# Two attention layers and two expert FFNs on one core: probabilities from block-diagonal queries, token-major experts, other load orders

## The reference

```
x = x + L0_xattn(layernorm(x), ctx, ctx)   # 32 query heads of 8 over 8 key heads; softmax(q k / sqrt(8)) v
x = x + L0_ffn(layernorm(x))               # 2 experts, 256 -> 1024 -> 256, leaky relu squared, the better expert
x = x + L1_xattn(layernorm(x), ctx)        # 16 heads of 16; q = x Wq, k and v = ctx Wkv; causal; then Wout
x = x + L1_ffn(layernorm(x))               # below
```

## Time and profile before

| | us |
|---|---|
| median of 3 runs (390.49 to 393.13) | 390.66 |
| the profiled execution | 389.83 |
| its span, first to last instruction | 387.8 |
| PE busy in it | 345.8 |
| DVE busy | 163.6 |
| ACT busy | 150.4 |
| POOL busy | 90.8 |

### The profile page before, as it was taken

The page is one execution under the profiler, slowest core; times in us unless marked ns, Lnnn a source line. Parts: engine busy times, 40 slices in busy tenths (PEclk is TensorE's granted clock), DMA queues, the critical chain, the costliest instruction groups (busy, mean ns, idle before and its releaser), DMA issues.

```text
span 387.8 us, 11733 instructions
## 1 busy us (share of the span) xinstructions
PE 345.8 (89%) x5105; PEld 282.2 (73%) x5105; DVE 163.6 (42%) x481; ACT 150.4 (39%) x349; POOL 90.8 (23%) x134
## 2 busy tenths in 40 slices
PE   2365679899998999899999999899999999996996
PEld 1234568777785887788788896788877888885784
DVE  4360473007730346088502684016364156327034
ACT  3012424332153332347142140433553666666452
POOL 6832423422342113142122430042100000200000
PEclk9999969989999999899999999999999999999899
DMA  3999000000000000000000000000000001000000
GB/s 87 288 401 365 8 1 3 3 3 2 0 3 3 3 3 2 3 3 3 0 5 3 0 1 2 5 0 2 0 2 27 3 1 32 0 0 15 14 1 29
DMA packets 7106, 12.84 MB, mean 33 GB/s; under 512 B 2576, under 2 KB 5392, under 8 KB 6288
## 3 DMA queue, kind: packets, MB, share of 16 engines
q1 hardware_dynamic: 7056, 12.10, 9.0%
HBM read 11.04 MB, written 1.05 MB: 31 GB/s over the span
## 4 chain that ended last, share of the span: by engine, by line
PE 82%; issue 6%; DVE 4%; SPq 3%; ACT 3%; POOL 1%; DMA 1%; DVEq 0%; POOLq 0%
PE Y L1243 27%; PE S L1243 27%; PE H L1243 24%; SPq L679 2%; PE S L1321 2%; DMA WKV<-in_wkv 1%; ACT PT L766 1%; PE S L1429 1%; PE S L1330 1%; POOL X L891 1%; SPq L674 1%; DVE XN L1002 0%; DVE MN L1030 0%; ACT YS L842 0%; PE S L1249 0%
## 5 line engine op out<-in xcount | busy, mean ns | idle before, releaser
L1243 PE MATMUL Y<-WP,A 128*128 128x256 f32 x256 | 64.0, 399 | 0.0
L1243 PE MATMUL H<-XT,WF 128*128 128x256 f32 x256 | 62.1, 391 | 0.0
L1243 PEld LDWEIGHTS Y<-WP,A 128*128 128x128 f32 x256 | 48.9, 199 | 8.1 <-issue 1.5
L1243 PEld LDWEIGHTS H<-XT,WF 128*128 128x128 f32 x256 | 47.9, 194 | 7.9 <-issue 1.5
L907 POOL TENSOR_TENSOR A<-R 128x512 f32<-128x512 f32 x32 | 33.2, 1040 | 61.9 <-PE Y L1243 57.5
L824 ACT ACTIVATE A<-H,B 128x256 f32<-128x256 f32 x84 | 35.6, 471 | 30.8 <-PE H L1243 30.7
L1243 PE MATMUL Y<-A,W 128*128 128x256 f32 x168 | 45.9, 383 | 0.4 <-DVE YG L1206 0.4
L1243 PE MATMUL H<-GH,W 128*128 128x256 f32 x168 | 44.6, 392 | 0.3 <-ACT GH L813 0.3
L796 ACT ACTIVATE R<-H 128x512 f32<-128x512 f32 x32 | 19.1, 598 | 47.4 <-POOL A L907 24.0
L1243 PEld LDWEIGHTS H<-GH,W 128*128 128x128 f32 x168 | 31.9, 195 | 5.7 <-issue 0.6
L1243 PEld LDWEIGHTS Y<-A,W 128*128 128x128 f32 x168 | 30.6, 192 | 6.3 <-issue 1.1
(11 more groups left out here) (171 smaller groups left out, 492.4 us busy)
## 6 DMA issues: line engine op xcount, KB each, us to landing
W<-in_w SPq DMA_DIRECT2D x2, 1344.0 KB, 9.2
WF<-in_wf SPq DMA_DIRECT2D x2, 1024.0 KB, 9.0
WP<-in_wp SPq DMA_DIRECT2D x2, 1024.0 KB, 11.1
X<-in_x SPq DMA_DIRECT2D x8, 128.0 KB, 7.5
out_dram<-X SPq DMA_DIRECT2D x8, 128.0 KB, 1.7
KR<-in_ctxT SPq DMA_DIRECT2D x4, 192.0 KB, 3.2
KR<-in_ctxT SPq DMA_DIRECT2D x8, 32.0 KB, 2.1
C<-in_ctx_in SPq DMA_DIRECT2D x1, 256.0 KB, 3.2
```

Of the source, the lines that this page charges most:

```text
L1243: return nc.tensor.matmul(o, a, b, start=start, stop=stop, skip_group_check=shared)
```

## The change

**Loads.** Rows 0 and 1 come first, then the context, rows 2 and 3 in one transfer, the keys of tiles 2 to 7, rows 4 to 7 in one transfer, and then the rest as before. The keys of tiles 0 and 1 are four transfers that ACT issues ahead of its own work.

**First attention.** After the scores POOL spreads the queries in the place of the keys (`k`, `queries0`, `Z0`), so that the second build takes 16 matmuls of 256 columns with the plain keys `KR0` as weights. The turned shifts are no longer copied by ACT: DVE multiplies them, from PSUM, with the 0/1 columns `place` into `MD0`, eight copies each of which keeps one of eight heads (`t`, `spread_shifts0`), and 8 matmuls of 512 columns with `ofbank0` add them, one for each bank, half and sequence.

**Second attention.** The same, with 4 shift and 8 score matmuls (`MD1`, `ofbank1`, `Z1`). ACT copies the keys out of PSUM, and POOL instead of DVE spreads the keys (`c`) and the queries (`k`).

**Second FFN.** The down products are token-major: `A1` stands in the array, 128 rows at a time, and the 128 columns of `W2` move, two matmuls a chunk. The gates are then a number per partition, and DVE multiplies and adds in one operation a tile. The selector matmuls, the three-part split `GS`, `YS` and `YG` are gone. The values at zero and the biases are one more product with the turned gates at the last expert (`ROWS0`), `zero_rows` makes that table with nine rows instead of eight, and a new stage `k` (`turn_sums`) turns the sum for `widen`. Constants for the selectors go, those for the new products come.

**Orders.** `COST`, `LOADED` and `URGENCY` have new numbers, so each engine's order is new. Two lines of it:

```diff
-    "ffn1": "v 38 -981 -81 -709; ln 661 727 727 220; x 460 425 492 992; i -16 -3 19 -711; r 695 118 935 143; "
+    "ffn1": "v -457 595 -279 -873; ln -550 -628 -623 -267; x 555 313 346 180; i 990 696 353 572; "
```

The core of the rest:

```diff
-            rows(0)
-            keys(0, 0, 1)
-            rows(1)
-            keys(1, 1, 2)
+            rows(0, 1)
+            rows(1, 2)
             sp.dma_start(C[:, :, :], ctx_in.rearrange("(t p) d -> p t d", p=P)).then_inc(ld_c, 16)
-            rows(2)
-            rows(3)
-            keys(2, 2, TILES)
+            rows(2, 4)
+            keys(sp, 1)
+            rows(4, 8)
             sp.dma_start(CT[:, :], ctxT).then_inc(ld_kv, 16)
...
+            keys(act, 0)
             run("act", h | {("attn0", "f"): probs0, ("attn0", "b"): values0, ("const", "e"): places0, ("attn1", "f"): probs1, ("attn1", "kv"): keys1,
...
+            def queries0(t, _):
+
+                filled(pool, "attn0", t, "h", 3)
+                read_out(pool, "attn0", t, "q", 0)
+                for c in range(DC):
+                    nc.gpsimd.tensor_tensor(Z0[:, t % 2, c, :, :], QT0[:, t % 2, c, :].unsqueeze(1).to_broadcast([P, 4, P]),
+                                            quarter0[:, :].unsqueeze(2).to_broadcast([P, 4, P]), ALU.mult).then_inc(qz_ready, 1)
...
+            def spread_shifts0(t, _):
+                b, done = filled(dve, "attn0", t, "t", 0)
+                nc.vector.tensor_tensor(MD0[:, t % 2, :, :], b[:, :].bitcast(bf16)[:, 0:P].unsqueeze(1).to_broadcast([P, 8, P]),
+                                        place[:, :].unsqueeze(2).to_broadcast([P, 8, P]), ALU.mult).then_inc(done, 1)
...
-                for j in range(8):
-                    for k in range(2):
-                        for r in range(2):
-                            i = 2 * r + k
-                            half = slice(r * S, (r + 1) * S)
-                            for bt in range(2):
-                                rows = slice(bt * S, (bt + 1) * S)
-                                mm(claims_[i][0][rows, j * S:(j + 1) * S], sel0[half, 8 * i + j, :], MT0[half, t % 2, rows],
-                                   start=(j == 0), stop=False, shared=True)
-                for j in range(8):
-                    c, r = divmod(j, 4)
+                for k in range(2):
+                    for r in range(2):
+                        half = slice(r * S, (r + 1) * S)
+                        for bt in range(2):
+                            rows = slice(bt * S, (bt + 1) * S)
+                            mm(claims_[2 * r + k][0][rows, :], ofbank0[half, 2 * r + k, :], MD0[half, t % 2, :, rows], stop=False,
+                               shared=True)
+                for c in range(DC):
                     for i, (b, done) in enumerate(claims_):
                         quarter = slice(32 * i, 32 * i + 32)
                         for bt in range(2):
                             rows = slice(bt * S, (bt + 1) * S)
-                            ins = mm(b[rows, j * S:(j + 1) * S], KZ0[quarter, t % 2, c, r, rows], QT0[quarter, t % 2, c, rows],
-                                     start=False, shared=True)
-                        if j == 7:
+                            ins = mm(b[rows, 4 * c * S:4 * (c + 1) * S], KR0[quarter, c, t * P + bt * S:t * P + (bt + 1) * S],
+                                     Z0[quarter, t % 2, c, :, rows], start=False, shared=True)
+                        if c == DC - 1:
                             ins.then_inc(done, 1)
...
-                ins = mm(at(*y)[:, 0:GT], W2[:, FIRST1[e] + c, :], A1[:, (g * NCH1 + i) % 4, :], start=(c == 0), stop=last_c)
+                for k in range(2):
+                    ins = mm(at(*y)[:, k * L:(k + 1) * L], A1[:, (g * NCH1 + i) % 4, k * P:(k + 1) * P], W2[:, FIRST1[e] + c, :],
+                             start=(c == k == 0), stop=last_c, shared=True)
                 if not last_c:
                     ins.then_inc(a1_used, 1)
                     return
-                if e < E1:
-                    if e == EXPERTS[1]:
-
-                        read_out(pe, "ffn1", g, "g", 0)
-                        if g == 0:
-                            pe.wait_ge(gates_const, 1)
-                    ins = mm(at(*y)[:, GT:2 * GT], selG[:, e, :], GTT[:, :])
+                if e == EXPERTS[-1]:
+
+                    read_out(pe, "ffn1", g, "g", 0)
+                    if g == 0:
+                        read_out(pe, "ffn1", 0, "z", 0)
+                    for k in range(2):
+                        ins = mm(at(*y)[:, (2 + k) * L:(3 + k) * L], GTT[:, k * P:(k + 1) * P], ROWS0[:, :], start=False, shared=True)
                 ins.then_inc(full["Y"], 1)
...
+                e = EXPERTS[j]
+                b, done = filled(dve, "ffn1", g, "y", j)
+                for k in range(2):
+                    ins = nc.vector.scalar_tensor_tensor(ACC[:, k, :], b[:, k * L:(k + 1) * L], gate[:, k, e:e + 1], ACC[:, k, :],
+                                                         ALU.mult, ALU.add)
+                    if k == 0 or j == E1:
+                        link(ins)
+                if j == E1:
+                    ins = nc.vector.tensor_tensor(flat(ACC[:, :, :]), b[:, GT:2 * GT], flat(ACC[:, :, :]), ALU.add)
+                ins.then_inc(done, 1)
```

385 lines of the change are left out of this document (195 added, 190 removed), and 43 rows, old and new, of the table URGENCY.

## The result

The changed kernel takes 370.36 us (median of 4 runs, 367.86 to 371.51) beside 390.89 for the kernel before: ratio 0.9455, 95% interval 0.9395 to 0.9515. Run again later it took 370.59, ratio 0.9452 (0.9403 to 0.9502). 374.5 was forecast. The medians differ by 20.5. The profiled execution took 371.51, the slowest of the four, with a span of 369.5, 18.3 less than the span of before; PE's busy time fell by 8.0 and the time in which it is not busy from 42.0 to 31.7.

What follows compares the result with a forecast made beforehand. PE, busy 345.8 of 387.8 us, was taken to bound the kernel. Terms -8.8 - 3.4 - 1.2 - 5.1 - 0.3 + 2.5 + 1 = -15.3 took 389.8 to 374.5; range 359 to 387.

Steps and rivals of the forecast that it cites:

- Head: Everything up to the first FFN: earlier key/value weights and cheaper rebuilt scores save 8.8 us net, bounds -4 and -13.
- The two marks: In the head, PE's first rebuilt scores end at 21.2 us and the second at 28.6, instead of 38.4 for the second.
- Rebuilt scores: Dense section: 1.60 us a tile in the first attention, 1.57 in the second; -3.4 and -1.2 in all.
- Issue idle: Dense section, first attention: with 40 records a tile instead of 192 the issue idle goes, -5.1; bounds 0 and -5.1.
- Spreads at nothing: Dense section: waits for POOL's query spread and DVE's shift spread cost nothing; up to 3.3 us a tile if cover fails.
- Narrow record: Second FFN: 336 down records of 128 columns at 0.1175 us each instead of 0.110, +2.5.
- The rest of the second FFN: Selector products go out; ROWS0 products, transposes of sums and f32 gate turns come in: net -0.3.
- Ends: Ends of the second FFN's four groups: sums pass PE and ACT again, gates may hold less; +1, from -4 to +4.
- The weight load: Rival, second FFN's down products: load no longer hides behind 128 columns, 0.182 a record, +22, 396 us; chance 0.05.
- POOL and DVE: Rival: POOL's added spreads and DVE's operations get in each other's way, +8, 383 us; chance 0.15.
- The stalls: Rival: fetch stalls stay, caught by the 64 value products; +5 to +9, 380 to 384 us; chance 0.1.
- The new orders: Rival: new orders also close other holes, with ends at -4, head -13, records 0.112; 363.5 us; chance 0.25.

Runs made afterwards that it cites:

- the wide form: The changed kernel with each down product of the second FFN as one product of 256 columns, 168 records instead of 336: 368.54 us, ratio 0.9451.
- The two runs: The changed kernel with first-attention score products cut into four of 64 columns, 416.39 us; the changed kernel with the old score products put back, 379.61.
- three kernels: The kernel before; the same with only the change's load order, 388.61 us; the changed kernel with the first attention's old score products, 379.61.

## Why the prediction was right, point by point

**Head.** Forecast -8.8, measured -9.1. The two marks came out (21.2 and 28.6 against 21.65 and 28.25), but by errors that cancelled, and partly by luck.

The load of the weights was issued at 6.99 as forecast, yet took 8.6 and not 4.9 us, and landed at 15.6 instead of 12, past the 14 that I had named as a sign of being wrong. I carried the duration of the earlier trace rows to another place. Fewer transfers stand ahead of it there (14 instead of 18), but they are larger and were issued in half the time: 2,560 KB by 6.99 instead of 2,048 KB by 12.05. It cost little (a weight load of PE waited 0.4 for it) only because the first maxima, which I let begin "at 9.78 as before", began at 11.15 (first keys), and the second queries were turned until 15.60 anyway.

What paid for the late maxima is the clock. I doubled PE's prices up to the second rebuilt scores. The granted clock of the change's profile rose to the higher level (2.4 GHz) at 20.5 us, in the first rebuilt scores, and fell at 27.4, in the second: each took 2.1 and not 3.2, and the projection's four records 1.01 at 15.60 but 0.55 at 22.31. That is the condition of my bound of -13, met for 7 us, and what it gave, the first keys (1.4) and a stretched split of the shifts (1.5, above) took back. In the second profile of the change the clock fell at 24.0 already, and the marks are 21.6 and 29.1. The zero rows, which I moved at the same cost, took 5.8 instead of 4.5 in their new place, at the lower level until 44.4.

**Rebuilt scores.** 1.60 and 1.57 forecast, 1.61 and 1.58 measured. The shapes of the earlier trace rows were the right ones. -4.2 instead of -3.4, since I priced all six tiles of the kernel before by one without a stall (2.17). The three with a stall took 2.31, 2.44 and 2.58 besides the stall itself.

**Issue idle.** Gone, and with it what the second attention's scores and the value products lost (0.7 and 0.4): -6.1. Putting the old products back brought back 1.6 in the dense section, and 3.6 in the head.

**Spreads at nothing.** Nearly: PE waits nowhere in the dense section for Z or MD. For the split of the second attention's shifts it waits 1.3 in three (MS, L1093), which I had no term for. My sign of PE over 95% busy in this section came true (98.7% from 48.6 to 330.8), but it could not tell right from wrong: the kernel before has 97.5% from 53.2 to 349.

**Narrow record.** The term was mis-sized: 0.111 and not 0.1175, so +0.3 by the undisturbed rows, +1.1 by the sums of the narrow and the wide form, instead of +2.5. The zero rows' 0.112 was the nearer row. The sustained 81 ns per matmul of 128 columns in the Trainium skill ("TensorE: Matmul & The Clock Gate", section "Back-to-back issue gap"), set against 53.3 for the columns alone, would have made an estimated +19; the runs here disagree.

**The rest of the second FFN.** I had the exchange of selectors for ROWS0, turns of the sums and f32 gates at -0.3; the sums give +0.2 (5.1 out, 5.3 in). The up products, for which I had no term, fell by 1.0.

**Ends.** The weakest step of the sum. The term said +1; the waits there came to 5.4 (sums 2.8, gates 1.6, ACC 0.5, GH 0.5) against 5.0 before (GS, ACC, YG, XT, GH), as forecast, but what follows them took 2.8 longer in the profiled execution. That is the clock, and it is a matter of the execution. The same kernel, profiled twice, PE after the same wait; from 332 to 336 us the granted clock was 0.50 in the first and 1.00 in the second:

```profile
332.22 0.66 PE L1511 MATMUL S<-identf,ACC 128*128 128x128 f32 x2 [1.38 <-DVE ACC L1238]
332.68 1.92 PE L1270 MATMUL Y<-CW,GX 128*128 128x256 f32 x4
```

```profile
332.73 0.41 PE L1511 MATMUL S<-identf,ACC 128*128 128x128 f32 x2 [1.38 <-DVE ACC L1238]
332.97 1.03 PE L1270 MATMUL Y<-CW,GX 128*128 128x256 f32 x4
```

**What I had not counted.** The products of the first FFN fell by 4.3 with no edit to them. In the kernel before they ran at the lower clock in three places, at their start (53.23) and behind the stalls that end at 76.19 and 158.55; by stretches of 10 us (PE busy, PEld, DVE, ACT, POOL, granted clock, DMA), before and after:

```profile
50.00:60.00 10.00, 9.28 (x63) 7.32 (x62) 8.13 (x29) 3.21 (x6) 2.83 (x5) 0.69 0.00 1
70.00:80.00 10.00, 8.42 (x215) 6.90 (x214) 0.52 (x1) 3.10 (x7) 4.33 (x5) 0.83 0.02 4
```

```profile
50.00:60.00 10.00, 10.00 (x106) 7.29 (x105) 5.48 (x16) 3.23 (x6) 6.85 (x8) 1.00 0.01 2
70.00:80.00 10.00, 9.61 (x100) 7.33 (x99) 7.45 (x17) 1.19 (x2) 7.10 (x10) 1.00 0.01 2
```

Against it stand the zero rows, 5.8 instead of 4.5 in their new place (counted in the head), and the 2.8 above. Without the row of the first FFN the sum would be -14.0, short of the forecast. A part of that row may be a price of the stalls that I left out, since two of the low stretches begin within 0.5 us of a stall's end. But none follows the stall that ends at 119.24, nor the one at 166.06 in the run with the old products. So I call it luck: no run shows more.

The mean granted clock of an execution is no higher than before (0.963 to 0.986, against 0.974 to 0.987 where the runs of before list it), but it hides the head. The profile has no granted clock ahead of the first rise, at 42.5 us in the kernel before and at 20.5 in the change, and the mean counts that time as full speed, though the products of the head took about twice their later time. Behind the start of the first FFN the low stretches only move: 49.4 to 56.2 (begun ahead of it), 76.7 to 80.1, 158.6 to 162.0 and 360.0 to 363.4 before, 331.1 to 338.0 and 361.9 to 365.3 after. So the clock explains a part of the head and the row of the first FFN, not the rest. The 4 us between runs of one kernel go with it (367.57 at 0.986, 371.92 at 0.963).

**The rivals.** The weight load did not become the bound, though the sign that I named for it came: loads are busy 43.4 us beside down products that take 39. POOL and DVE do get in each other's way, far from +8: at one place of the head by 1.5, and of the 1.3 above 0.17 stands behind a stretched cast (0.85 at 273.88, against 0.17). The stalls did not stay in the value products. The new orders closed some holes and opened others; no run has the new products in the old orders, so what the orders alone are worth is not shown.

## What to carry to other kernels

Price a new product by the row of the same shape on both operands, and a narrower form by the narrow row that exists, not by the recorded length of its weight load. A load's duration belongs to its place in the queue; count the bytes that are ahead of it on every queue, and when they were issued. A stall that keeps its place in the program and ends behind a packet of the instruction queue is bought off by fewer instructions. A wait that is closed shows the next one, as three of the last runs did. Compare executions at the same granted clock before you credit an edit with 3 us.

## What was not expected of the hardware

Products of 64 columns were three times as slow in one order as in another. With four products of one quarter behind each other a record takes 47 ns (48.1 us for 1024), with the quarters taking turns 14 (14.5 for 1024, above). The two runs also differ in which operand stands in the array, so the order is the likely cause and not the only difference:

```profile
L1270 PE MATMUL S<-Z,KR 32*64 32x64 f32 x1024 | 48.1, 250 | 0.0
```

The Trainium skill, "TensorE: Matmul & The Clock Gate", Part 3 on packing small matmuls, has products on distinct row groups of the array run at the same time; the 14 ns with the quarters taking turns agree.

Each of the 16 issue stalls of three kernels ends 1.26 to 1.59 us after a 16 KB packet of the instruction queue; the eight in the kernel before make up its 11.6 us.

A weight load recorded at 191 ns does not occupy PE for that long: 336 of them followed each other every 111 to 116 ns.

DVE's cast stood still for all of POOL's memory set, 1.81 beside 1.80. The Trainium skill, "SBUF — State Buffer", section "Who interferes with whom", states that casts in the two-port mode and POOL's operations lock each other out for a whole instruction; the trace agrees. The second operation, with two inputs from SBUF, was held by the key spread (0.99) and had its 0.23 once the memory set was over.

After the same wait of 1.38 us the granted clock fell in one execution and not in another.
